# Layer norms and the expert threshold computed on GpSimd instead of ScalarE and VectorE

## The chip, the core and the metric

One NeuronCore of one Trainium2 chip runs the whole program. The metric is the device time of one execution in microseconds; before, the median of three runs is 1113.73 us. TensorE is called PE here, VectorE DVE, ScalarE ACT, GpSimd POOL and SyncE SP, as in the profile.

## The reference

64 sequences of 64 tokens, 128 wide, go through three residual blocks. Each block first takes the layer norm of its input.

```python
def _layernorm(x, axis=-1, eps=1e-05):
    m = jnp.mean(x, axis=axis, keepdims=True)
    v = jnp.var(x, axis=axis, keepdims=True)
    return (x - m) / jnp.sqrt(v + eps)
...
x = x + _L0_xattn_ref(_layernorm(x), ctx_768, Wq, Wk, Wv, Wo, bo)      # cross attention, 16 heads of 64
x = x + _L0_attn_ref(_layernorm(x), Wp, bp, Wv, Wo)                    # causal tree attention, 16 heads
x = x + _L0_ffn_ref(_layernorm(x), Wq, bq, K1, K2, W_up, W_down)       # product-key experts
...
    vals, best = jax.lax.top_k(all_scores, TOPK)       # _L0_ffn_ref: 8 heads, the 10 best of 100 sums
    scores = jax.nn.softmax(vals, axis=-1)
    h = jax.nn.gelu(h, approximate=False) * scores
    out = jnp.einsum('bshk,bshkd->bsd', h, w_up)
```

## The kernel before

The 4096 tokens are worked on as 32 tiles of 128 tokens (two sequences). The work on a tile is cut into about 130 named steps: `x.*` and `y.*` are the cross attention, `t.*` the tree attention, `k.*` the keys of the expert layer and `e.*` its eight heads of 1024 expert sums. Each engine runs its own dictionary of steps, `PE_ORDER`, `ACT_ORDER`, `DVE_ORDER`, `POOL_ORDER`, `SP_ORDER`, written out by hand: the key is the step, the number its lag. Loop `i` of `run` (line 157) goes through the dictionary and does each step for tile `i` minus its lag. So in a full loop every engine works on six or so tiles at once, in a fixed order, and each step waits only for the semaphores of the steps that it needs. There are 32 + 7 loops, of which the first and last ones are thin.

The layer norm, three times a tile (`x`, `t`, `k`):

- DVE takes mean and variance, with the helper `stats` (bn_stats L857, bn_aggr L860, adding eps L862): in `x.stats`, in `y.res` (behind the residual add L906) and in `t.res` (behind L939).
- POOL's `x.root`, `t.root`, `k.root` raise the variance to -0.5 (L1058), wait for that, and multiply it by minus the mean (L1061). Both numbers lie in `rstd`.
- ACT's `x.norm`, `t.norm`, `k.norm` (L686) apply them as scale and bias to the 128x128 tile.
- PE transposes the result (`x.turn` L327, `t.turn` L452, `k.turn` L525).

Behind `k.turn`: ACT's `k.high` (L760) and DVE's `k.low` (L876) split the transposed tile in two fp16 parts, PE's `k.key` makes 512 key scores, DVE's `k.top` takes 16 times the eight largest (L951) and `k.split` (L963, L965) shifts and splits the scores. ACT's `k.shift` (L766) copies them, `e.gelu` (L785 to L787) loads a function table, makes the gelu and loads the first table back, `x.w0`, `x.w1`, `x.w2` (L622) copy queries, `t.sb` (L715) copies the tile that `t.turn` transposed. PE's `x.s0` (L377) needs `x.w0` and `x.w1`; `t.pv` (L462 to L464) comes behind it and feeds ACT's `t.pexp` (L722) and DVE's `t.path` (L919), from which POOL's `t.feat` (L1100, L1104) makes features for PE's `t.fturn`.

The threshold: DVE's `k.cand` finds the 16 best candidates per head with max (L978), match_replace (L983) and max (L988), adds the tenth and the eleventh after the first (L991) and halves the sum (L993) into `cut`. Eight masks `e.w0` to `e.w7` on DVE (L1012) keep the expert weights whose sum is at least `cut`; POOL adds them up in `e.a1` to `e.a7` (L1120). ACT's `k.eb` (L773) takes exponentials of the ten best.

POOL also normalises the attention probabilities, `x.n0` to `x.n3` (L1071), and makes the inner candidates, `k.inner` (L1083, L1089).

Of the kernel before, what the change touches and what calls it, by code (L numbers as in the profile page):

```python
# [29 lines left out]
def build(nc, a):  # L30
# [3 lines left out]
    with ctx:  # L34
# [3 lines left out]
        def sem(name):  # L38
# [36 lines left out]
        rstd = sb("rstd", [128, 3, 2, 2])  # L75
# [53 lines left out]
            dve_path dve_tnorm dve_top dve_split dve_cand dve_zsum pool_inner pool_feat""".split()}  # L129
# [531 lines left out]
        def _(act):  # L661
# [20 lines left out]
            def norm(name, i, src, slots, dst, root, turn):  # L682
                def step(t):
                    act.wait_ge(s[root], t + 1)
                    after(act, turn, t - 2)
                    done(name, act.activation(dst[:, t % 2, :], src[:, t % slots, :], ACT.Identity,  # L686
                                              scale=rstd[:, i, t % 2, 0:1], bias=rstd[:, i, t % 2, 1:2]))
                return step
            steps["x.norm"] = norm("x.norm", 0, x, 2, xn, "x.root", "x.turn")
            steps["t.norm"] = norm("t.norm", 1, x2, 2, xn2, "t.root", "t.turn")  # L690
            steps["k.norm"] = norm("k.norm", 2, x3, 4, xn3, "k.root", "k.turn")

# [107 lines left out]
            steps["x.norm"](0)  # L800
# [4 lines left out]
            run(steps, ACT_ORDER, begun=(("x.norm", 0),), once={ACT_VO: setup_vo, ACT_KEYS: setup_keys})  # L805

        @block.vector
        def _(dve):
# [32 lines left out]
            def setup_down():  # L841
# [9 lines left out]
                                 (("dve_top", 16), ("dve_split", 1), ("dve_cand", 4), ("dve_zsum", 1)))  # L851
# [12 lines left out]
            def x_stats(t):  # L864
                dve.wait_ge(s["ld.x"], 16 * (t + 1))
                after(dve, "x.root", t - 2)
                stat_chain["x.stats"].begin(t)
                stats("x.stats", 0, x[:, t % 2, :], t)
# [30 lines left out]
            def add_cross(t):  # L899
                dve.wait_ge(s["y.out"], t + 1)  # L900
                dve.wait_ge(s["ld.xr"], 16 * (t + 1))
                after(dve, "t.norm", t - 2)
                after(dve, "t.root", t - 2)
# [65 lines left out]
            def candidates(t):  # L969
# [4 lines left out]
                after(dve, "e.w7", t - 4)  # L974
# [14 lines left out]
                lc.link(ins)  # L989
                lc.wait()  # L990
                lc.link(dve.tensor_tensor(cut[:, t % 4, :], best[:, :, TOPK], best[:, :, TOPK + 1], ALU.add))  # L991
                lc.wait()
                done("k.cand", dve.tensor_scalar_mul(cut[:, t % 4, :], cut[:, t % 4, :], 0.5))  # L993
# [49 lines left out]
        def _(pool):  # L1043
# [49 lines left out]
            steps["k.inner"] = inner_sums  # L1093

# [44 lines left out]
    "t.norm": 4, "x.w1": 3, "x.w2": 3, "t.sb": 4, "t.pexp": 4, "t.v": 4, "k.eb": 5, "x.e0": 3, "k.lnz": 5,  # L1139
# [12 lines left out]
    "e.a7": 6, "x.root": 2, "t.feat": 4, "x.n0": 3, "x.n2": 3, "e.a1": 5, "x.n1": 3, "x.n3": 3, "e.a2": 5,  # L1152
    "k.root": 4, "e.a3": 5, "e.a4": 5, "e.a5": 5, "k.inner": 4, "e.a6": 5, "t.root": 3,
# [60 lines left out]
```

## Time and profile before

| | us |
|---|---|
| median of three runs (lowest, highest) | 1113.73 (1105.69, 1114.01) |
| the profiled execution, its own time | 1110.33 |
| its span | 1106.9 |
| busy PE / PE weight loads | 981.0 (89%) / 782.8 (71%) |
| busy ACT | 903.5 (82%) |
| busy DVE | 888.9 (80%) |
| busy POOL | 826.6 (75%) |
| DMA engines, mean | 25 GB/s |

The span is the time from the first to the last instruction of one profiled execution; the execution's own time is 3.4 us more. "Busy" is the time in which an engine had an instruction running, waits left out. The TensorE clock granted is full (tenths 9 or 10) from 100 us to 1020 us.

### The profile page before, as it was taken

The numbers are of one execution on the slowest core, as the hardware profiler recorded it, in microseconds if no ns is written. First come the engines' busy times: TensorE is split into PE (matmuls) and PEld (weight loads), VectorE is DVE, ScalarE is ACT, GpSimd is POOL, SyncE is SP. The second block draws the span as 40 slices with busy tenths as digits, with TensorE's granted clock in tenths as the row PEclk, the third lists the DMA queues.
The fourth block names the chain that finished last, engine by engine and source line by source line (L and its number), as shares of the span: only waits on it lengthen the run. The fifth ranks groups of instructions, "written<-read, shape, count | busy, mean of one in ns | idle before, by whom it ended". The sixth has DMA issues, their size and how long they took to land. (4 is left out here: it accounts for less than half of the span.)

```text
span 1106.9 us, 36026 instructions
## 1 busy us (share of the span) xinstructions
PE 981.0 (89%) x12440; PEld 782.8 (71%) x12440; DVE 888.9 (80%) x2941; ACT 903.5 (82%) x2223; POOL 826.6 (75%) x871
## 2 busy tenths in 40 slices
PE   6869899999999999999999999999999999999865
PEld 5657677777777777777777777777777777777533
DVE  3266898888888888888888888888888888888773
ACT  3557888889898888898988889898888898988752
POOL 0316778788777788877778788777788887777765
PEclk9988999999999999999999999999999999999875
DMA  6000011110001111010011110001111010010000
GB/s 165 13 20 9 20 26 26 26 26 20 15 20 26 25 26 26 20 25 15 19 26 26 25 26 20 17 17 26 26 25 26 21 26 14 20 24 19 13 13 5
DMA packets 70369, 27.27 MB, mean 25 GB/s; under 512 B 47312, under 2 KB 69936, under 8 KB 70192
## 3 DMA queue, kind: packets, MB, share of 16 engines
q1 hardware_dynamic: 69152, 24.58, 9.5%
q8 instruction: 103, 1.69, 0.7%
q14 instruction: 74, 0.61, 0.2%
q10 hardware_dynamic: 1040, 0.39, 0.1%
HBM read 14.47 MB, written 2.10 MB: 15 GB/s over the span
## 5 line engine op out<-in xcount | busy, mean ns | idle before, releaser
L1120 POOL TENSOR_TENSOR wsum<-wsum,mw 128x1024 f32<-128x1024 f32 x192 | 453.1, 2360 | 5.6
L1012 DVE SCALAR_TENSOR_TENSOR mw<-psF,cut,ew 128x1024 f32<-128x1024 f32 x256 | 324.9, 1280 | 38.9 <-ACT ew L795 38.8
L795 ACT ACTIVATE ew<-psF,lnz 128x1024 f32<-128x1024 f32 x256 | 281.5, 1126 | 13.5 <-PE psF L589 10.7
L1071 POOL TENSOR_TENSOR p<-p,rrow 128x512 f32<-128x512 f32 x128 | 131.5, 1038 | 98.4 <-DVE rrow L894 98.4
L705 ACT ACTIVATE p<-psXT,negmax 128x128 f32<-128x128 f32 x512 | 181.8, 383 | 2.2 <-DVE negmax L885 2.1
L589 PE MATMUL psF<-sel,usT 128*128 128x512 f16 x512 | 159.0, 394 | 19.1 <-DVE mw L1012 16.8
L377 PEld LDWEIGHTS psXT<-cT,q 96*128 96x128 f32 x1024 | 131.5, 195 | 60.2 <-DVE q L626 40.1
L377 PE MATMUL psXT<-cT,q 96*128 96x128 f32 x1024 | 142.5, 283 | 31.8 <-DVE q L626 25.9
L705 ACT ACTIVATION_READ_ACCUMULATOR p<-psXT,negmax 128x1 f32 x512 | 115.1, 225 | 0.0
L418 PE MATMUL psXT<-pT,c 128*32 128x384 f32 x768 | 104.7, 501 | 0.6 <-ACT pT L622 0.6
L885 DVE TENSOR_REDUCE negmax<-psXT 128x4 f32<-128x512 f32 x128 | 85.9, 671 | 22.2 <-PE psXT L377 19.4
L420 PE MATMUL psXT<-pT,c 128*32 128x128 f32 x768 | 102.8, 278 | 0.0
L312 PE MATMUL psXT<-xnT,qk 128*96 128x128 f16 x512 | 91.6, 222 | 3.4 <-DVE xnT L876 1.8
L439 PE MATMUL psXT<-vo,uT 128*128 128x128 f32 x768 | 92.6, 277 | 0.0
L314 PE MATMUL psXT<-xnT,qk 128*96 128x128 f16 x512 | 91.4, 222 | 0.0
L313 PE MATMUL psXT<-xnT,qk 128*96 128x128 f16 x512 | 91.4, 222 | 0.0
L439 PEld LDWEIGHTS psXT<-vo,uT 128*128 128x128 f32 x768 | 88.3, 192 | 0.0
L766 ACT ACTIVATE cand<-psXT 128x512 f32<-128x512 f32 x32 | 19.1, 598 | 80.6 <-DVE us L965 80.6
L1058 POOL TENSOR_TENSOR rstd<-mv,halfneg 128x1 f32<-128x1 f32 x96 | 52.8, 550 | 43.0 <-DVE mv L862 42.6
L1120 POOL TENSOR_TENSOR wsum<-mw 128x1024 f32<-128x1024 f32 x32 | 75.5, 2360 | 10.8 <-DVE mw L1012 10.8
L611 PE MATMUL psF<-wup,gT 128*128 128x128 f32 x512 | 70.4, 294 | 11.7 <-DVE mw L1012 10.3
L611 PEld LDWEIGHTS psF<-wup,gT 128*128 128x128 f32 x512 | 64.2, 204 | 18.5 <-DVE mw L1012 16.9
(134 smaller groups left out, 2373.4 us busy)
## 6 DMA issues: line engine op xcount, KB each, us to landing
cT<-cT_dram SPq DMA_DIRECT2D x32, 96.0 KB, 2.0
c<-c_dram SPq DMA_DIRECT2D x32, 96.0 KB, 2.1
x<-x_dram SPq DMA_DIRECT2D x32, 64.0 KB, 2.4
xr<-x_dram SPq DMA_DIRECT2D x32, 64.0 KB, 1.9
y_dram<-y SPq DMA_DIRECT2D x32, 64.0 KB, 1.5
wqT<-wqT_dram SPq DMA_DIRECT2D x1, 512.0 KB, 5.0
wo<-wo_dram SPq DMA_DIRECT2D x1, 512.0 KB, 6.6
wdT<-wdT_dram SPq DMA_DIRECT2D x1, 512.0 KB, 3.5
```

Source lines behind the costliest of these rows:

```text
L312: pe.matmul(out, left[:, 0, :], right[:, 0, :], start=not open_group, stop=False)
L377: mm = pe.matmul(bank[BANK[f"x.s{k}"]][:, i * M:i * M + M], q[:, b, h:h + 2, :].rearrange("c h q -> c (h q)"), cT[:, t % 2, b, :], start=T ...
L418: pe.matmul(to[32 * j:32 * j + 32], cols, probs[:, :, 0:3, :], start=True, stop=True, tile_position=(0, 32 * j))
L420: mm = pe.matmul(to[96:128, :, j, :], cols, probs[:, :, 3, :], start=True, stop=True, tile_position=(0, 96))
L439: mm = pe.matmul(out, uT[:, i, :, :].rearrange("c b q -> c (b q)"), vo[:, i, :], start=False, stop=(i == XH3 - 1))
L589: mm = pe.matmul(bank[BANK[f"e.s{h}"]][:, j * 512:j * 512 + 512], usT[:, t % 4, h, :], sel[:, j * 512:j * 512 + 512], start=True, stop=True)
L611: mm = pe.matmul(bank[BANK["e.out"]][:, 0:D], gT[:, c, :], wup[:, c, :], start=(c == 0), stop=(c == EC - 1))
L705: ins = act.activation(p[:, k, i, :], bank[BANK[f"x.s{k}"]][:, i * M:i * M + M], ACT.Exp, bias=negmax[:, k, i:i + 1], accum_out=rowsum[:, ...
L795: done(f"e.x{h}", act.activation(ew[:, h % NEW, :], bank[BANK[f"e.s{h}"]], ACT.Exp, bias=lnz[:, t % 4, h:h + 1]))
L1012: done(f"e.w{h}", dve.scalar_tensor_tensor(out=mw[:, h % NMW, :], in0=bank[BANK[f"e.s{h}"]], scalar=cut[:, t % 4, h:h + 1], in1=ew[:, h % ...
L1071: done(f"x.n{k}", pool.tensor_tensor(p[:, k, :, :], p[:, k, :, :], rrow[:, k, :].unsqueeze(2).to_broadcast([128, 4, M]), ALU.mult))
L1120: done(f"e.a{h}", pool.tensor_tensor(wsum[:, t % 2, :], mw[:, 0, :] if h == 1 else wsum[:, t % 2, :], mw[:, h % NMW, :], ALU.add))
```

## The change

The three ACT steps `x.norm`, `t.norm`, `k.norm` and the three POOL steps `x.root`, `t.root`, `k.root` become three POOL steps `x.norm`, `t.norm`, `k.norm`: the power as before, a wait for it, and one tensor_scalar that subtracts the mean from the 128x128 tile and multiplies by the root. They stand where the roots stood. The add and the halving of the threshold leave DVE's `k.cand` and become a POOL step `k.cut`, between `e.a7` and `x.norm`, one loop behind `k.cand`. The masks wait for `k.cut` besides. The first `x.norm` is no longer issued ahead of the setup on ACT.

```diff
         @block.scalar
-            def norm(name, i, src, slots, dst, root, turn):
-                def step(t):
-                    act.wait_ge(s[root], t + 1)
-                    after(act, turn, t - 2)
-                    done(name, act.activation(dst[:, t % 2, :], src[:, t % slots, :], ACT.Identity,
-                                              scale=rstd[:, i, t % 2, 0:1], bias=rstd[:, i, t % 2, 1:2]))
-                return step
...
         @block.vector
             def candidates(t):
...
-                after(dve, "e.w7", t - 4)
+                after(dve, "k.cut", t - 1)
...
                 for h in range(FH):
                     ins = dve.max(best[:, h, 8:16], cand2[:, h, :])
-                lc.link(ins)
-                lc.wait()
-                lc.link(dve.tensor_tensor(cut[:, t % 4, :], best[:, :, TOPK], best[:, :, TOPK + 1], ALU.add))
-                lc.wait()
-                done("k.cand", dve.tensor_scalar_mul(cut[:, t % 4, :], cut[:, t % 4, :], 0.5))
+                done("k.cand", ins)
...
             def mask(h):
                 def step(t):
                     dve.wait_ge(s[f"e.x{h}"], t + 1)
+                    dve.wait_ge(s["k.cut"], t + 1)
...
         @block.gpsimd
-            def root(name, i, stats, norm):
+            def layer_norm(name, i, src, slots, dst, stats, turn):
+
                 def step(t):
                     pool.wait_ge(s[stats], t + 1)
-                    after(pool, norm, t - 2)
-                    l = root_chain[name]
+                    after(pool, turn, t - 2)
+                    l = norm_chain[name]
                     l.begin(t)
                     l.link(pool.tensor_tensor(rstd[:, i, t % 2, 0:1], mv[:, i, t % 2, 1:2], halfneg[:], ALU.pow))
                     l.wait()
                     pool.nop(nofuse=True)
-                    done(name, pool.tensor_scalar(rstd[:, i, t % 2, 1:2], mv[:, i, t % 2, 0:1],
-                                                  rstd[:, i, t % 2, 0:1], -1.0, ALU.mult, ALU.mult))
+                    done(name, pool.tensor_scalar(dst[:, t % 2, :], src[:, t % slots, :], mv[:, i, t % 2, 0:1],
+                                                  rstd[:, i, t % 2, 0:1], ALU.subtract, ALU.mult))
...
+            def middle(t):
+
+                pool.wait_ge(s["k.cand"], t + 1)
+                after(pool, "e.w7", t - 4)
+                lcut.begin(t)
+                pool.nop(nofuse=True)
+                lcut.link(pool.tensor_tensor(cut[:, t % 4, :], best[:, :, TOPK], best[:, :, TOPK + 1], ALU.add))
+                lcut.wait()
+                done("k.cut", pool.tensor_scalar_mul(cut[:, t % 4, :], cut[:, t % 4, :], 0.5))
+            steps["k.cut"] = middle
...
 POOL_ORDER = {
-    "e.a7": 6, "x.root": 2, "t.feat": 4, "x.n0": 3, "x.n2": 3, "e.a1": 5, "x.n1": 3, "x.n3": 3, "e.a2": 5,
-    "k.root": 4, "e.a3": 5, "e.a4": 5, "e.a5": 5, "k.inner": 4, "e.a6": 5, "t.root": 3,
+    "e.a7": 6, "k.cut": 5, "x.norm": 2, "t.feat": 4, "x.n0": 3, "x.n2": 3, "e.a1": 5, "x.n1": 3, "x.n3": 3,
+    "e.a2": 5, "k.norm": 4, "e.a3": 5, "e.a4": 5, "e.a5": 5, "k.inner": 4, "e.a6": 5, "t.norm": 3,
 }
```

The order of the instructions on each engine, in a full loop. ACT before, around `k.norm`: two exponentials of expert sums (`ew`), the norm of the third block (`xn`, L686), a copy of the mix (`uT`) and `k.high` (`xn3T`).

```order
L795 ACTIVATE ew<-psF,lnz 128x1024 [waits e_w1,k_lnz,e_s5]
L795 ACTIVATE ew<-psF,lnz 128x1024 [waits e_w2,k_lnz,e_s6]
L686 ACTIVATE xn<-x,rstd 128x128 [waits k_turn,k_root]
L622 ACTIVATE uT<-psXT 128x6x64 [waits y_out,y_m1]
L760 ACTIVATE xn3T<-psXT 128x128 [waits e_hid,k_key,k_turn]
L622 ACTIVATE uT<-psXT 128x6x64 [waits y_out,y_m3]
```

ACT now, at the same place:

```order
L784 ACTIVATE ew<-psF,lnz 128x1024 [waits e_w1,k_lnz,e_s5]
L784 ACTIVATE ew<-psF,lnz 128x1024 [waits e_w2,k_lnz,e_s6]
L622 ACTIVATE uT<-psXT 128x6x64 [waits y_out,y_m1]
L749 ACTIVATE xn3T<-psXT 128x128 [waits e_hid,k_key,k_turn]
L622 ACTIVATE uT<-psXT 128x6x64 [waits y_out,y_m3]
```

Only the norm has gone; the rest follows in the same order. ACT before, around `t.norm`: the table load behind the gelu, the query copies `x.w0`, `x.w1`, `x.w2` (`q`), the norm between the first two, and `t.sb` (`xn2T`).

```order
L787 ACT_TABLE_LOAD
L622 ACTIVATE q<-psXT 96x4x2x64 [waits x_s2,x_s0,x_q0]
L686 ACTIVATE xn<-x,rstd 128x128 [waits t_turn,t_root]
L622 ACTIVATE q<-psXT 96x4x2x64 [waits x_s2,x_s0,x_q1]
L622 ACTIVATE q<-psXT 96x4x2x64 [waits x_s3,x_s1,x_q2]
L715 ACTIVATE xn2T<-psXT 128x128 [waits t_pv,t_turn]
```

ACT now, at the same place:

```order
L776 ACT_TABLE_LOAD
L622 ACTIVATE q<-psXT 96x4x2x64 [waits x_s2,x_s0,x_q0]
L622 ACTIVATE q<-psXT 96x4x2x64 [waits x_s2,x_s0,x_q1]
L622 ACTIVATE q<-psXT 96x4x2x64 [waits x_s3,x_s1,x_q2]
L704 ACTIVATE xn2T<-psXT 128x128 [waits t_pv,t_turn]
```

`x.w1` now stands directly behind `x.w0`. POOL before, from `e.a6` to `t.feat`: sums of masked weights (`wsum`), the roots of the second and the first block (`rstd`), and the first instruction of the features (`path`).

```order
L1120 TENSOR_TENSOR wsum<-wsum,mw 128x1024 [waits e_w6,e_a5]
L1058 TENSOR_TENSOR rstd<-mv,halfneg 128x1 [waits t_norm,y_res]
L1061 TENSOR_SCALAR rstd<-mv,rstd 128x1 [waits pool_t_root]
L1120 TENSOR_TENSOR wsum<-wsum,mw 128x1024 [waits e_w7,e_a6]
L1058 TENSOR_TENSOR rstd<-mv,halfneg 128x1 [waits x_norm,x_stats]
L1061 TENSOR_SCALAR rstd<-mv,rstd 128x1 [waits pool_x_root]
L1100 TENSOR_SCALAR path<-path 128x80 [waits t_path,t_fturn]
```

POOL now, at the same place:

```order
L1117 TENSOR_TENSOR wsum<-wsum,mw 128x1024 [waits e_w6,e_a5]
L1044 TENSOR_TENSOR rstd<-mv,halfneg 128x1 [waits t_turn,y_res]
L1047 TENSOR_SCALAR xn<-x,mv,rstd 128x128 [waits pool_t_norm]
L1117 TENSOR_TENSOR wsum<-wsum,mw 128x1024 [waits e_w7,e_a6]
L1087 TENSOR_TENSOR cut<-best 128x8 [waits k_cand,e_w7]
L1089 TENSOR_SCALAR cut<-cut 128x8 [waits pool_cut]
L1044 TENSOR_TENSOR rstd<-mv,halfneg 128x1 [waits x_turn,x_stats]
L1047 TENSOR_SCALAR xn<-x,mv,rstd 128x128 [waits pool_x_norm]
L1097 TENSOR_SCALAR path<-path 128x80 [waits t_path,t_fturn]
```

The second instruction of each root has become one over the 128x128 tile, and the two of `k.cut` stand between `e.a7` and `x.norm`. On PE the order is the same; on DVE only the two threshold instructions are gone.

## Rows read from the trace of the kernel before

**Rows 1.** Busy us (instructions) in one loop: PE, PEld, DVE, ACT, POOL; clock, DMA.

```profile
502.53:534.41 31.88, 29.43 (x388) 23.69 (x387) 27.37 (x91) 27.90 (x71) 25.79 (x27) 1.00 0.10 23
```

**Rows 2.** Timeline of ACT, first and last full loops: start, us, instruction, [idle before <-releaser].

```profile
119.70 0.22 ACT L722 ACTIVATE psXT<-psXT 128x80 f32<-128x80 f32 x1 [1.22 <-PE psXT L464]
...
1012.24 0.22 ACT L722 ACTIVATE psXT<-psXT 128x80 f32<-128x80 f32 x1 [1.22 <-PE psXT L464]
```

**Rows 3.** Timeline of ACT, one full loop, 502.5 to 536 us.

```profile
519.60 0.51 ACT L686 ACTIVATE xn<-x,rstd 128x128 f32<-128x128 f32 x1
...
520.59 0.28 ACT L760 ACTIVATE xn3T<-psXT 128x128 f16<-128x128 f32 x1
...
526.51 0.60 ACT L766 ACTIVATE cand<-psXT 128x512 f32<-128x512 f32 x1 [2.43 <-DVE us L965]
...
531.25 0.48 ACT L686 ACTIVATE xn<-x,rstd 128x128 f32<-128x128 f32 x1
531.64 1.06 ACT L622 ACTIVATE q<-psXT 96x512 f32<-96x512 f32 x2
...
534.09 0.22 ACT L722 ACTIVATE psXT<-psXT 128x80 f32<-128x80 f32 x1 [1.22 <-PE psXT L464]
```

**Rows 4.** Timeline of DVE, the same loop.

```profile
518.75 1.28 DVE L1012 SCALAR_TENSOR_TENSOR mw<-psF,cut,ew 128x1024 f32<-128x1024 f32 x1 [0.42 <-ACT ew L795]
...
522.57 1.66 DVE L951 MAX8 top<-psXT 128x8 f32<-128x32 f32 x16
...
525.79 0.69 DVE L965 SCALAR_TENSOR_TENSOR us<-psXT,us 128x512 f16<-128x512 f32 x1
...
533.05 0.17 DVE L991 TENSOR_TENSOR cut<-best 128x8 f32<-128x8 f32 x1
```

**Rows 5.** Timeline of PE, the same loop.

```profile
515.71 0.30 PE L513 MATMUL psXT<-ident,actx 128*128 128x128 f32 x1 [0.29 <-DVE actx L929]
...
520.25 0.30 PE L525 MATMUL psXT<-ident,xn 128*128 128x128 f32 x1 [0.26 <-ACT xn L686]
520.39 0.59 PE L589 MATMUL psF<-sel,usT 128*128 128x512 f16 x2
...
531.57 0.22 PE L314 MATMUL psXT<-xnT,qk 128*96 128x128 f16 x1
...
532.36 1.13 PE L377 MATMUL psXT<-cT,q 96*128 96x128 f32 x8 [0.18 <-ACT q L622]
```

**Rows 6.** Timeline of POOL, the same loop.

```profile
518.42 0.55 POOL L1058 TENSOR_TENSOR rstd<-mv,halfneg 128x1 f32<-128x1 f32 x1 [0.25 <-DVE mv L862]
...
529.83 0.55 POOL L1058 TENSOR_TENSOR rstd<-mv,halfneg 128x1 f32<-128x1 f32 x1
...
533.82 0.27 POOL L1061 TENSOR_SCALAR rstd<-mv,rstd 128x1 f32<-128x1 f32 x1 [0.17 <-POOL rstd L1058]
536.19 0.26 POOL L1100 TENSOR_SCALAR path<-path 128x80 f32<-128x80 f32 x1 [2.11 <-DVE path L919]
```

**Rows 7.** Groups by form, POOL: busy us, mean ns of one, idle before and releaser.

```profile
L1071 POOL TENSOR_TENSOR p<-p,rrow 128x512 f32<-128x512 f32 x128 | 131.5, 1038 | 98.4 <-DVE rrow L894 98.4
...
L1100 POOL TENSOR_SCALAR path<-path 128x80 f32<-128x80 f32 x32 | 8.3, 258 | 75.3 <-DVE path L919 75.3
L1104 POOL TENSOR_TENSOR feat<-feat,path 128x16 f32<-128x16 f32 x32 | 7.9, 248 | 2.7
```

**Rows 8.** The chain that ended last, in order of time, thin loops: start, us, what.

```profile
1058.24 0.02 issue
1058.26 0.30 DVE x L939
...
1060.45 0.50 ACT xn L686
...
1073.64 0.18 DVE cut L991
```

**Rows 9.** All masks of the run: ns min/median/max, first and last start.

```profile
L1012 DVE SCALAR_TENSOR_TENSOR mw<-psF,cut,ew x256: 1271/1283/1286, 90.2 to 1091.5; 128x1024 f32<-128x1024 f32 x128
```

More of the change, by code:

```diff
@@ L74, in build @@
         mv = sb("mv", [128, 3, 2, 2])
-        rstd = sb("rstd", [128, 3, 2, 2])
+        rstd = sb("rstd", [128, 3, 2, 1])
         xn = sb("xn", [128, 2, D])
@@ L128, in build @@
             setup_ps setup_sb key_sb parts_done split_done
-            dve_path dve_tnorm dve_top dve_split dve_cand dve_zsum pool_inner pool_feat""".split()}
+            dve_path dve_tnorm dve_top dve_split dve_cand dve_zsum pool_inner pool_cut pool_feat""".split()}
         block = ctx.enter_context(nc.Block())
@@ L680, in _ @@
             copies(act, steps, ACT_ORDER)
-            def norm(name, i, src, slots, dst, root, turn):
-                def step(t):
-                    act.wait_ge(s[root], t + 1)
-                    after(act, turn, t - 2)
-                    done(name, act.activation(dst[:, t % 2, :], src[:, t % slots, :], ACT.Identity,
-                                              scale=rstd[:, i, t % 2, 0:1], bias=rstd[:, i, t % 2, 1:2]))
-                return step
-            steps["x.norm"] = norm("x.norm", 0, x, 2, xn, "x.root", "x.turn")
-            steps["t.norm"] = norm("t.norm", 1, x2, 2, xn2, "t.root", "t.turn")
-            steps["k.norm"] = norm("k.norm", 2, x3, 4, xn3, "k.root", "k.turn")
             def x_high(t):
@@ L799, in _ @@
                 steps[f"e.x{h}"] = exp_sums(h)
-            steps["x.norm"](0)
             for j in range(4):
@@ L804, in _ @@
                                ACT.Copy, scale=QKSCALE).then_inc(own["setup_sb"], 1)
-            run(steps, ACT_ORDER, begun=(("x.norm", 0),), once={ACT_VO: setup_vo, ACT_KEYS: setup_keys})
+            run(steps, ACT_ORDER, once={ACT_VO: setup_vo, ACT_KEYS: setup_keys})
         @block.vector
@@ L850, in _ @@
             ltop, lsp, lc, lz = (Chain(dve, own[n], k) for n, k in
-                                 (("dve_top", 16), ("dve_split", 1), ("dve_cand", 4), ("dve_zsum", 1)))
+                                 (("dve_top", 16), ("dve_split", 1), ("dve_cand", 2), ("dve_zsum", 1)))
             stat_chain = {n: Chain(dve, sem("dve_" + n.replace(".", "_")), k)
@@ L865, in x_stats @@
                 dve.wait_ge(s["ld.x"], 16 * (t + 1))
-                after(dve, "x.root", t - 2)
+                after(dve, "x.norm", t - 2)
                 stat_chain["x.stats"].begin(t)
@@ L902, in add_cross @@
                 after(dve, "t.norm", t - 2)
-                after(dve, "t.root", t - 2)
                 l = stat_chain["y.res"]
@@ L1048, in _ @@
             steps = {}
-            root_chain = {n: Chain(pool, sem("pool_" + n.replace(".", "_")), 1) for n in ("x.root", "t.root", "k.root")}
+            lcut = Chain(pool, own["pool_cut"], 1)
+            norm_chain = {n: Chain(pool, sem("pool_" + n.replace(".", "_")), 1) for n in ("x.norm", "t.norm", "k.norm")}
             li, lf = (Chain(pool, own[n], k) for n, k in (("pool_inner", 1), ("pool_feat", DEPTH)))
-            def root(name, i, stats, norm):
+            def layer_norm(name, i, src, slots, dst, stats, turn):
                 def step(t):
                     pool.wait_ge(s[stats], t + 1)
-                    after(pool, norm, t - 2)
-                    l = root_chain[name]
+                    after(pool, turn, t - 2)
+                    l = norm_chain[name]
                     l.begin(t)
@@ L1060, in step @@
                     pool.nop(nofuse=True)
-                    done(name, pool.tensor_scalar(rstd[:, i, t % 2, 1:2], mv[:, i, t % 2, 0:1],
-                                                  rstd[:, i, t % 2, 0:1], -1.0, ALU.mult, ALU.mult))
-                return step
-            steps["x.root"] = root("x.root", 0, "x.stats", "x.norm")
-            steps["t.root"] = root("t.root", 1, "y.res", "t.norm")
-            steps["k.root"] = root("k.root", 2, "t.res", "k.norm")
+                    done(name, pool.tensor_scalar(dst[:, t % 2, :], src[:, t % slots, :], mv[:, i, t % 2, 0:1],
+                                                  rstd[:, i, t % 2, 0:1], ALU.subtract, ALU.mult))
+                return step
+            steps["x.norm"] = layer_norm("x.norm", 0, x, 2, xn, "x.stats", "x.turn")
+            steps["t.norm"] = layer_norm("t.norm", 1, x2, 2, xn2, "y.res", "t.turn")
+            steps["k.norm"] = layer_norm("k.norm", 2, x3, 4, xn3, "t.res", "k.turn")
             def norm(k):
@@ L1138 @@
 ACT_ORDER = {
-    "t.norm": 4, "x.w1": 3, "x.w2": 3, "t.sb": 4, "t.pexp": 4, "t.v": 4, "k.eb": 5, "x.e0": 3, "k.lnz": 5,
[4 rows of a table removed]
[4 rows of a table added]
 }
```

8 rows, old and new, of the table ACT_ORDER are left out of this document.

## The prediction

> **What bounds the kernel now.** I read the busy shares first. In a full loop of 31.88 us PE works 29.43, DVE 27.37, ACT 27.90 and POOL 25.79 [rows 1]: no engine is full, so the period is set by a ring of waits, and the question is which ring and what the change takes from it. The activation `t.pexp` starts at 119.70 and again at 1012.24 [rows 2]; 892.54 us at 31.88 are 28 full loops, which carry nearly the whole effect.
>
> Next I read the four compute engines over one loop, 502.5 to 534.4, and asked at each idle gap what ended it. The ring:
> - ACT has no gap from `t.pexp` (at 502.2, and 534.09 a loop later) to `k.high` at 520.59 [rows 3]. On the way stands `k.norm` at 519.60.
> - `k.high` frees DVE's `k.low` and PE's `k.key`; DVE goes on with `e.w6`, the 16 maxima of `k.top` at 522.57, and ends `k.split` at 525.79 + 0.69 = 526.48 [rows 4].
> - ACT has waited 2.43 us for just that, and starts `k.shift` at 526.51 [rows 3]. Two table loads, the gelu, `x.w0`, `t.norm` at 531.25 and `x.w1` at 531.64 follow without a gap.
> - PE's `x.s0` waits 0.18 us for `x.w1` and starts at 532.36 [rows 5]; `t.pv` follows, ACT waits 1.22 us for it and starts `t.pexp` at 534.09 [rows 3]. The ring closes after 31.88 us.
>
> POOL is not in the ring: it stands idle for 2.11 us before `t.feat` [rows 6]. The third norm, `x.norm`, stands behind `k.high` and before the 2.43 us gap, so it costs nothing today.
>
> **The change part by part.**
>
> *ACT loses three activations a loop.* In a busy queue one takes the distance between neighbours: 531.64 - 531.25 = 0.39 us, though each is listed with about 0.5 [rows 3]. `x.norm` gives nothing (the 2.43 us gap becomes longer). The other two lie on the ring.
>
> *At `k.norm`* the activation frees 0.39 us, but `k.high` also needs PE's transpose `k.turn`. That waited 0.26 us for the normalised tile and ran at 520.25 [rows 5]; before it PE's work has followed on since `t.cturn` at 515.71 (behind a 0.29 us wait for DVE), and nothing of that moves. So `k.turn` can come at 519.99, 0.26 earlier. Behind it `e.s7`, now at 520.39, waits for the mask `e.w5`, which ends at 518.75 + 1.28 = 520.03 [rows 4]; with the 0.14 us that PE shows between a releaser's end and its matmul, `e.s7` starts at 520.17, 0.22 earlier. `x.p0`, `k.key` and so `k.top` follow. I take 0.22 us here, not 0.39. Is the tile there in time? POOL starts the root at 518.42 [rows 6]; 0.55 for the power, 0.17 wait and 0.35 for the new instruction (below) end at 519.49, and PE could start at 519.63. It is, with 0.36 to spare.
>
> *At `t.norm`* the full 0.39 us goes: `x.w1` starts 0.22 + 0.39 = 0.61 earlier, and `x.s0` could start at 531.75. The others it needs: PE's queries end at 531.57 + 0.22 = 531.79 [rows 5], shifted to 531.57; the transpose `t.turn` starts then, and a matmul behind a transpose starts 0.14 later (520.25 to 520.39), so 531.71. That is just not the bound. `t.turn` needs POOL's `t.norm`: 529.83, plus 0.08 from `k.norm`, plus 0.55 + 0.17 + 0.35 = 530.98 [rows 6], 531.12 on PE. It holds with 0.4 us to spare. So `t.pexp` comes 0.61 us earlier each loop.
>
> *The new POOL instruction* (128x128, one tensor input, two scalars in memory) is not in the trace. The nearest row is the 128x80 scalar form, 258 ns; with both inputs tensors, 128x16 costs 248 and 128x512 costs 1038, that is 1.6 ns an element, so 48 elements more than 80 make at most 0.33 [rows 7]. Bounds: 0.26 below, 0.43 above (248 and 112 elements more of the two-tensor kind), and 1.04, far away, the 128x512 row itself. I take 0.35, nearest the first row; against the 128x1 form at 533.82 that it replaces (0.27 [rows 6]) this is 0.08 more, three times a loop.
>
> That a norm on POOL costs no more than a small instruction speaks against a general warning. The Trainium skill, "GPSIMD Engine Reference", section "Engine selection", sends elementwise work to VectorE, GpSimd being about half as fast with two inputs, but calls one-input work roughly line-rate. At that page's 1.2 GHz the 128 elements are 0.11 us beyond the fixed cost, an estimate; no run so far shows the instruction. By it the sum above stays.
>
> *The threshold on POOL:* an 8-element add (at most 0.25, the 128x16 row), a 0.17 wait and a scalar form (0.26): 0.68 us [rows 6, 7]. It stands after `e.a7`, ending about 533.2, where the maxima of `k.cand`, ending at 533.0, are just done; shifted by 0.22 they are earlier still. The next reader, mask `e.w2`, stands eight DVE instructions further on, so this wait costs nothing. Behind it on POOL are `x.norm` (used a loop later) and `t.feat`. POOL's last small instruction ended at 533.82 + 0.27 = 534.09; now 0.24 + 0.68 later, 535.01. `t.feat`, at 536.19 because DVE's path comes then, will want to start at 535.58. So 0.57 us remain. That is the cover of all the POOL work; what is added beyond it makes `t.feat` late and then `t.fturn` on PE.
>
> *DVE loses* the add and the multiplication of the threshold, two of 0.17 from 533.05, with their waits some 0.4 us [rows 4]. The next, the maxima `x.x0`, needs `x.s0`, whose 1.13 us end at 533.49 [rows 5], so they hid nothing but 0.06 us of waiting. In the loop they are worth 0. The eight masks get a third wait (`k.cut`); where DVE already stands with three waits, at the residual add behind `t.out`, it starts 0.02 us after its releaser all the same [rows 8]. I take 0, at worst 0.05 at two or three masks beside the ring.
>
> The shared memory interface is the other worry. Masks that read one tile in SBUF and one in PSUM take 1271 to 1286 ns over all 256, beside a POOL that works 25.79 of 31.88 us [rows 1, 9]: no contention shows. The Trainium skill, "GPSIMD Engine Reference", section "Key points", expects it only with two SBUF inputs or a 2-port mode of VectorE; by that rule the new POOL reads could stretch VectorE's small SBUF operations, which are some 0.3 us each and few. That would change the sum by less than 0.1 us a loop.
>
> *Outside the full loops.* At the end, `k.norm` is in the chain (0.50 at 1060.45) and so are the two threshold instructions (from 1073.64 on, 0.39 with the gaps) [rows 8]. The first saves 0.50 + 0.02 - 0.08 = 0.4, the second 0.4. At the start some three thin loops hold one or both norms: 1.1 us by estimate.
>
> **Sum:** 28 x 0.61 = 17.1, plus 0.8 and 1.1: 19.0 us. The profiled execution took 1110.33 us, 3.4 outside its span and all; less 19.0 that is 1091.3. The median of the three runs is 1113.73, 3.4 above the profiled run, so in its terms 1094.7. I predict 1095. The three runs reach from 1105.69 to 1114.01; about 1%, 11 us, is what a measurement can tell from no change.
>
> **The rivals.**
> 1. *Only one of the two savings arrives.* For it: within 0.3 us of the ring run PE's route (0.26 idle before `k.turn`, 0.18 before `x.s0`) and the start of `x.s0` is only 0.04 clear of PE's. Against: I followed these and found them in step. If `k.norm` gives nothing, 28 x 0.39 + 1.9 = 12.8 us, 1101; if `t.norm` gives nothing, 28 x 0.22 + 1.9 = 8.1 us, 1106. Chance 0.22, about half of it under 1%.
> 2. *Slower: POOL becomes the bound.* One mechanism: the new instruction is much dearer, because of its two scalars in memory. The extra d counts twice up to `t.norm`: POOL's tile came at 530.82 against ACT's at 531.74, so from d = 0.46 (an instruction of 0.73 us) `t.turn` is no earlier than now. It counts three times up to `t.feat`, where 2.11 - 0.68 = 1.43 us were free, to be passed at d = 0.48. At 1.04 us (d = 0.77) `t.feat` is 3 x 0.77 - 1.43 = 0.9 late, less some 0.3 of room before `t.fturn`: 0.6 x 28 = 17 us slower, 1130. Against: the 128x80 form at 258 ns. The Trainium skill, "GPSIMD Engine Reference", section "Engine selection", with its preference for VectorE speaks the same way as this rival. Chance 0.08.
> 3. *No effect:* some chain that I missed holds the period at 31.88, for instance masks handed over later by the third wait, which runs beside the ring through `x.r0` and POOL's `x.n1` to PE's `x.p1`. Only the ends gain: 1112. Chance 0.10.
>
> **How the numbers follow.** The forecast has 0.60 and is faster by 1.7%. With half of rival 1 (0.11) faster has 0.70; same is the other half and most of rival 3, 0.20; slower is rival 2 and a rest of 0.02, 0.10. The range: the forecast's own is 1088 to 1100 (0.45 to 0.8 us a loop, the latter if PE overlaps more than I allow). It is widened to 1084 because one run of before was 8 us under the median, and to 1111 for rival 1 and a part of rival 3.
>
> **What would show it.** Right: loops of 31.27 us between two `t.pexp`; `k.turn` at 0.26 less distance from `t.cturn`; POOL's norm instruction near 0.35 us; ACT down by 3 x 0.49 busy a loop, with its wait before `k.shift` grown by 0.4 to 0.6; POOL's gap before `t.feat` down from 2.11 to about 0.6. Wrong: a gap on PE before `t.turn` or `t.fturn` that POOL ends, a POOL norm above 0.7 us, or DVE masks starting more than 0.05 us behind ACT.

## The result, and the profile after

The changed kernel takes 1102.05 us (median of 20 runs), the kernel before 1109.43 (20 runs): a ratio of 0.9942, 95% interval 0.9927 to 0.9958. It is faster by 0.6%, where I had forecast 1.7% (1095 us), and by less than the 1% that I had called the limit of "no change". The three runs that I had to predict from had a median 4 us above that of the twenty.

The first row to read is the one I had to estimate: the new instruction, all 96 of them.

```profile
L1047 POOL TENSOR_SCALAR xn<-x,mv,rstd x96: 797/797/1027, 4.7 to 1052.3; 128x128 f32<-128x128 f32 x96
```

Its columns are ns min/median/max, first and last start. I had taken 350 ns, with 0.26 to 0.43 as near bounds. The timeline of ACT has `t.pexp` twice in a typical full loop; [rows 3] is its counterpart.

```profile
211.42 0.22 ACT L711 ACTIVATE psXT<-psXT 128x80 f32<-128x80 f32 x1 [1.34 <-PE psXT L464]
...
243.07 0.22 ACT L711 ACTIVATE psXT<-psXT 128x80 f32<-128x80 f32 x1 [1.34 <-PE psXT L464]
```

The loop is 31.65 us, not 31.27. Busy time in that loop (columns as in [rows 1]):

```profile
211.42:243.07 31.65, 29.48 (x387) 23.57 (x386) 26.96 (x90) 26.98 (x66) 27.85 (x30) 1.00 0.10 23
```

ACT lost 0.92 us and POOL gained 2.06 against [rows 1]. I had forecast 1.47 for ACT, three times the listed 0.49; neighbouring activations overlap, so each takes away less busy time than its own length. Who is late is on the timeline of PE at `k.turn`, `t.turn` and `x.s0`:

```profile
229.13 0.30 PE L525 MATMUL psXT<-ident,xn 128*128 128x128 f32 x1
...
241.12 0.30 PE L452 MATMUL psXT<-ident,xn 128*128 128x128 f32 x1 [0.45 <-POOL xn L1047]
241.35 1.13 PE L377 MATMUL psXT<-cT,q 96*128 96x128 f32 x8
```

`t.turn` waits 0.45 us for POOL, one of the rows that I had named as the sign of failure. (`x.s0`, which waited 0.18 us for ACT in [rows 5], has no wait here.) The timeline of POOL, the counterpart of [rows 6], says why.

```profile
213.63 0.26 POOL L1097 TENSOR_SCALAR path<-path 128x80 f32<-128x80 f32 x1
...
227.46 0.56 POOL L1044 TENSOR_TENSOR rstd<-mv,halfneg 128x1 f32<-128x1 f32 x1
228.19 0.80 POOL L1047 TENSOR_SCALAR xn<-x,mv,rstd 128x128 f32<-128x128 f32 x1 [0.18 <-POOL rstd L1044]
228.96 7.25 POOL L1117 TENSOR_TENSOR wsum<-wsum,mw 128x1024 f32<-128x1024 f32 x3
236.16 0.32 POOL L1069 TENSOR_TENSOR tops<-top 128x80 f32<-128x80 f32 x1
236.56 0.61 POOL L1075 TENSOR_TENSOR cand<-tops 128x32 f32<-128x32 f32 x3
237.13 2.35 POOL L1117 TENSOR_TENSOR wsum<-wsum,mw 128x1024 f32<-128x1024 f32 x1
239.44 0.56 POOL L1044 TENSOR_TENSOR rstd<-mv,halfneg 128x1 f32<-128x1 f32 x1
240.18 0.80 POOL L1047 TENSOR_SCALAR xn<-x,mv,rstd 128x128 f32<-128x128 f32 x1 [0.18 <-POOL rstd L1044]
```

From `k.norm` to the end of `t.norm` POOL has no gap but the 0.18 us between a norm's two instructions. Its last longer gap lies before `x.n3`, which waits 0.65 us for DVE's reciprocal L882 and starts 12.6 us after `t.pexp`. So POOL is now part of the ring: `x.n3`, `e.a2`, `k.norm`, three sums, `k.inner`, `e.a6`, `t.norm`, then PE's `t.turn`, `x.s0`, `t.pv` and ACT's `t.pexp`. The 2.11 us that POOL idled before `t.feat` are gone (no bracket at 213.63).

**Where the time went, by the profiled executions.** I split each span at the third `t.pexp` and at the one 28 loops later. Before: 119.70, 892.54, 94.66 us. After: 115.65, 887.98, 94.17. So of 9.1 us, 4.6 came from the 28 loops (0.16 each on average, since a few of them are longer than 31.65), 4.05 from the thin loops at the start and 0.5 from the end. The start is not to be put down to the norms. In its last thin loop PE ran at a mean granted clock of 0.90 before and 0.98 after:

```profile
85.73:119.70 33.97, 29.65 (x363) 23.66 (x362) 25.91 (x89) 28.19 (x70) 25.76 (x27) 0.90 0.09 20
```

```profile
83.91:115.65 31.74, 26.98 (x363) 21.25 (x362) 25.57 (x87) 26.82 (x67) 25.98 (x25) 0.98 0.09 21
```

The first is before, the second after. This stretch differs by some us between executions of the same instructions: the kernel before, run again, reached its third `t.pexp` at 118.46 us, where it had been 119.70, and the kernel of the probe below, which is the changed one up to its end, at 117.55, where that had been 115.65. So I compare the kernels by their full loops.

### The profile page after: what moved, and what is told of

Read it like the earlier page. It is cut to its first block and busy times, and to the rows that moved or that the text cites. A ratio compares the mean times of both kernels' runs of the same rounds, so it can differ in the third digit from the quotient of the medians.

```text
span 1097.8 us, 35846 instructions
## 1 busy us (share of the span) xinstructions
PE 980.3 (89%) x12440; PEld 778.7 (71%) x12440; DVE 876.6 (80%) x2877; ACT 873.4 (80%) x2127; POOL 892.2 (81%) x935
## 5 line engine op out<-in xcount | busy, mean ns | idle before, releaser
L1047 POOL TENSOR_SCALAR xn<-x,mv,rstd 128x128 f32<-128x128 f32 x96 | 76.9, 801 | 17.3 <-POOL rstd L1044 17.3
L622 ACT ACTIVATE pT<-psXT 128x512 f32<-128x512 f32 x128 | 74.1, 605 | 9.6 <-PE psXT L396 8.8
```

## The experiments

Loop is the distance of two `t.pexp` in the commonest full loop, mean the average over the same 28. Both are read from one profiled execution of each kernel. The expectations below speak of `arz`: in the kernel before, DVE stood idle for 0.25 us ahead of this reciprocal (L927) in 25 of its 32 loops, and the profile names nobody that it waited for. The last two runs are about this stall.

| kernel | loop, us | mean, us | ratio to before, 95% interval |
|---|---|---|---|
| before | 31.88 | 31.88 | |
| changed | 31.65 | 31.71 | 0.9942 (0.9927 to 0.9958) |
| threshold alone on POOL | 31.69 | 31.72 | 0.9972 (0.9947 to 0.9998) |
| norms alone on POOL | 32.33 | 32.42 | 1.0164 (1.0107 to 1.0221) |
| changed, POOL reordered | 31.20 | 31.26 | 0.9816 (0.9767 to 0.9865) |
| changed, cheaper norm instruction | 31.01 | 31.05 | 0.9753 (0.9707 to 0.9800) |
| norms alone, threshold sum a reduction | 32.07 and 32.85 | 32.42 | 1.0159 (1.0110 to 1.0208) |
| norms alone, threshold one reduction | 31.70 | 31.76 | 0.9963 (0.9952 to 0.9975) |
| reordered, `t.norm` back on ACT | 31.58 | 31.62 | one run, 1103.00 us |
| reordered, norm by an addition | 31.04 | 31.05 | 0.9775 (0.9755 to 0.9795) |
| before again | 31.85 | 31.86 | one run, 1106.45 us |
| before, one empty DVE instruction a loop | 31.72 | 31.75 | one run, 1105.93 us |

**The threshold alone.** The kernel before, with `k.cut` of the change and its waits in the masks.

```diff
-    "e.a7": 6, "x.root": 2, "t.feat": 4, ...
+    "e.a7": 6, "k.cut": 5, "x.root": 2, "t.feat": 4, ...
```

> The kernel before with the threshold alone moved to POOL; the norms stay on ACT. Theory A (the changed kernel's gain comes from the two norm activations that left ACT, and was capped by POOL's 0.80 us norms): the ring still runs through ACT's k.norm and t.norm, so a full loop stays at 31.88 us, or 31.72 if the 0.25 us stall of DVE before arz, which is in most loops of the kernel before and in none of the changed one, depends on DVE's instruction stream; the time is the same within 0.5%. Theory B (it is the shorter DVE that gave the gain, the norms gave nothing): the loop is 31.65 us as in the changed kernel, and the ratio to before is 0.994.

Measured: a loop of 31.69 us, ratio 0.9972, and the 25 stalls before `arz` are gone. The loop fits A with the stall gone (31.72); its distance from B's 31.65 is too small to decide. The last run, which takes only the stall out of the kernel before, has 31.72 as well: the threshold by itself, the third wait of the masks included, neither gives nor costs anything that these loops show. The averages, 31.72 here and 31.71 in the changed kernel, say more: the norms on POOL, as the change writes them, added next to nothing to this kernel's loops.

**The norms alone.** The changed kernel with the two threshold instructions back on DVE.

```diff
-                done("k.cand", ins)
+                lc.link(ins)
+                lc.wait()
+                lc.link(dve.tensor_tensor(cut[:, t % 4, :], best[:, :, TOPK], best[:, :, TOPK + 1], ALU.add))
+                lc.wait()
+                done("k.cand", dve.tensor_scalar_mul(cut[:, t % 4, :], cut[:, t % 4, :], 0.5))
```

> The changed kernel with the threshold back on DVE. Theory A: POOL's ring, from e.a2 over k.norm, three sums, k.inner, e.a6 and t.norm to PE's t.turn, sets the loop with or without k.cut, because k.cut stands outside it: 31.65 us without the stall before arz, 31.82 with it, PE idle 0.4 us before t.turn on POOL's account; ratio to before 0.994 to 0.998. Theory B: without the shorter DVE the loop is back at 31.88.

Both missed: 32.33 us, slower than before by 1.6%. The cause is one instruction that neither theory had looked at, DVE's add L978 (all 32; columns as above). The second row is the same add in the kernel before.

```profile
L978 DVE TENSOR_TENSOR cut<-best x32: 171/1395/1478, 82.4 to 1087.5; 128x8 f32<-128x8 f32 x32
```

```profile
L991 DVE TENSOR_TENSOR cut<-best x32: 170/171/275, 82.7 to 1073.6; 128x8 f32<-128x8 f32 x32
```

An add of 8 elements in each partition takes 1.4 us; before it took 0.17 [rows 4]. The timelines of DVE and of POOL at that place:

```profile
699.50 1.13 DVE L978 TENSOR_TENSOR cut<-best 128x8 f32<-128x8 f32 x1
700.67 0.17 DVE L980 TENSOR_SCALAR cut<-cut 128x8 f32<-128x8 f32 x1
```

```profile
698.25 2.36 POOL L1108 TENSOR_TENSOR wsum<-wsum,mw 128x1024 f32<-128x1024 f32 x1
```

POOL's sum `e.a7` ends at 700.61, the add at 700.63. So it is in the other loops: in 30 of the 32 the add starts 0.98 to 1.45 us before the end of `e.a7` and ends 0.02 to 0.04 us after it. Before, `e.a7` ran from 28.57 to 30.92 us after `t.pexp` and the add began at 30.85: it came just as the sum ended. Three of its 32 adds began 0.18 to 0.25 us before the end of the sum and took 0.20, 0.26 and 0.28 us, ending with it, so the first sign of this stood in the trace that I predicted from. The norms move `e.a7` to 30.18 and its end to 32.5, on top of the add. The maxima behind the add are then late, ACT waits for them (0.33 us at `x.e0`), and the ring grows.

**POOL reordered.** Two steps of the changed kernel stand elsewhere.

```diff
-    "e.a7": 6, "k.cut": 5, "x.norm": 2, "t.feat": 4, "x.n0": 3, "x.n2": 3, "e.a1": 5, "x.n1": 3, "x.n3": 3,
-    "e.a2": 5, "k.norm": 4, "e.a3": 5, "e.a4": 5, "e.a5": 5, "k.inner": 4, "e.a6": 5, "t.norm": 3,
+    "e.a7": 6, "k.cut": 5, "t.feat": 4, "x.norm": 2, "x.n0": 3, "x.n2": 3, "e.a1": 5, "x.n1": 3, "x.n3": 3,
+    "e.a2": 5, "k.norm": 4, "e.a3": 5, "e.a4": 5, "e.a5": 5, "k.inner": 4, "t.norm": 3, "e.a6": 5,
```

> The changed kernel with two POOL steps in other places: t.norm before e.a6 in place of behind it, x.norm behind t.feat in place of before it. Nothing is computed otherwise. Theory A: t.norm's tile is ready some 2 us earlier, so PE no longer waits for POOL before t.turn, and the ring is the one that I forecast for the change: 0.56 to 0.61 us less than 31.72, a loop of 31.1 to 31.2 us; 28 loops by 0.5 us from 31.65 are 14 us, so about 0.982 of before. Theory C (PE's own queue or a DVE handoff is what holds 31.65, POOL only looks late): the loop stays at 31.5 to 31.7 and the ratio at 0.994.

Measured: 31.20 us and 0.9816, as theory A had it. Theory C is out. POOL at `t.norm`:

```profile
675.48 0.56 POOL L1044 TENSOR_TENSOR rstd<-mv,halfneg 128x1 f32<-128x1 f32 x1 [0.48 <-DVE mv L850]
676.22 0.80 POOL L1047 TENSOR_SCALAR xn<-x,mv,rstd 128x128 f32<-128x128 f32 x1 [0.18 <-POOL rstd L1044]
```

The tile is ready at 27.8 us after `t.pexp` (649.21), where it was 29.6; `t.turn` follows PE's queries at 29.12 without a wait. The two exchanges were made together; what `x.norm` behind `t.feat` gives by itself no run shows.

**The price of the instruction.** Eight forms on scratch tiles at the end of the program, where nothing else runs on POOL.

```diff
...
+            form(lambda: pool.tensor_scalar(pb[:, 0:128], pa[:, 0:128], m, r, ALU.subtract, ALU.mult))
+            form(lambda: pool.tensor_scalar(pb[:, 0:128], pa[:, 0:128], m, r, ALU.mult, ALU.add))
+            form(lambda: pool.tensor_scalar(pb[:, 0:128], pa[:, 0:128], r, -1.0, ALU.mult, ALU.mult))
+            form(lambda: pool.tensor_scalar(pb[:, 0:128], pa[:, 0:128], 2.0, -1.0, ALU.mult, ALU.add))
...
```

> The changed kernel, and when POOL has nothing more to do it runs eight forms of instruction three times each on scratch tiles, with a wait between them; they compute nothing that is used. It measures what the forecast took at 0.35 us. Theory P (two scalars in memory cost by the element, some 5 to 6 ns): two memory scalars take 0.80 us over 128 elements, 0.5 over 64, 1.4 over 256, and immediates 0.3. Theory S (it is the subtraction): multiply-and-add with two memory scalars takes 0.35 and only subtract-and-multiply 0.80. Theory F (a fixed cost of two scalars in memory): 0.8 at every width from 1 to 256.

The rows of the tile that they write, in that order, then the first form at 64, 1 and 256 columns, and a two-tensor multiplication:

```profile
L1138 POOL TENSOR_SCALAR pb<-pa,mv,rstd x3: 792/793/802, 1092.0 to 1093.8; 128x128 f32<-128x128 f32 x3
L1139 POOL TENSOR_SCALAR pb<-pa,mv,rstd x3: 447/447/448, 1094.7 to 1095.8; 128x128 f32<-128x128 f32 x3
L1140 POOL TENSOR_SCALAR pb<-pa,rstd x3: 366/371/373, 1096.4 to 1097.3; 128x128 f32<-128x128 f32 x3
L1141 POOL TENSOR_SCALAR pb<-pa x3: 297/298/298, 1097.8 to 1098.5; 128x128 f32<-128x128 f32 x3
L1142 POOL TENSOR_SCALAR pb<-pa,mv,rstd x3: 572/574/580, 1098.9 to 1100.3; 128x64 f32<-128x64 f32 x3
L1143 POOL TENSOR_SCALAR pb<-pa,mv,rstd x3: 364/370/399, 1101.0 to 1101.9; 128x1 f32<-128x1 f32 x3
L1144 POOL TENSOR_SCALAR pb<-pa,mv,rstd x3: 1220/1246/1246, 1102.4 to 1105.1; 128x256 f32<-128x256 f32 x3
L1145 POOL TENSOR_TENSOR pb<-pa,rstd x3: 398/399/399, 1106.4 to 1107.3; 128x128 f32<-128x128 f32 x3
```

Theory S, in kind: at 128 columns and with the same two memory scalars, subtract-and-multiply takes 793 ns and multiply-and-add 447, though S had 350 for the latter. The memory scalars cost about 75 ns each at this width (298, 371, 447); the form with the subtraction costs 3.4 ns an element ((1246 - 370) / 255). F is out by the 370 ns at one column, P by the 447: it had the dear price for any form with two memory scalars. What this probe leaves open is whether the subtraction is dear or any form that adds before it multiplies; a run below settles it.

**The cheaper form in the kernel.** The norms compute x * root + mean, not the layer norm; it is a measure of time.

```diff
-                    ... src[:, t % slots, :], mv[:, i, t % 2, 0:1], rstd[:, i, t % 2, 0:1], ALU.subtract, ALU.mult)
+                    ... src[:, t % slots, :], rstd[:, i, t % 2, 0:1], mv[:, i, t % 2, 0:1], ALU.mult, ALU.add)
```

> The changed kernel in which the three POOL norms multiply by the root and add the mean (447 ns in the probe) where they subtract the mean and multiply by the root (796 ns). This is another value than the layer norm, and so a measure of time alone: the instruction costs about what I had forecast. Theory A (the forecast failed by this one price): k.norm and t.norm are 0.35 us each shorter, t.norm's tile comes 0.70 us earlier at PE where the changed kernel waits 0.45 for it, so POOL leaves the ring and the loop falls from 31.65 to 31.2 us, the ratio to before to 0.983. Theory C (something else also caps the changed kernel at this order of POOL): the loop stays above 31.45.

31.01 us and 0.9753: A, and more than its 31.2. With this one price changed, POOL's place in the order is as in the changed kernel and the loop is 0.64 us shorter. The reordered kernel had stopped at 31.20 because its `k.norm` still held `k.turn`, which came 17.75 us after `t.pexp`; here it comes at 17.54.

**One input in place of two.** To see what holds DVE in the norms-alone kernel, the sum became a reduction.

```diff
-                lc.link(dve.tensor_tensor(cut[:, t % 4, :], best[:, :, TOPK], best[:, :, TOPK + 1], ALU.add))
+                lc.link(dve.reduce_sum(cut[:, t % 4, :], best[:, :, TOPK:TOPK + 2], AX.X))
```

> The kernel with only the norms on POOL, where DVE's threshold add took 1.28 us in place of 0.18 and the loop 32.33 us. Here DVE makes the same sum as a reduction over the two neighbouring values, one input where the add has two. Theory K (a DVE instruction with two inputs in SBUF waits until POOL's running two-input instruction is over): the reduction takes about 0.2 us beside the same POOL work, and the loop falls to what POOL's ring gives, 31.65 to 31.8 us, ratio 0.994 to 0.999. Theory L (DVE there waits for something else, or any DVE instruction on these addresses is held): the reduction too takes over 1 us and the loop stays at 32.3.

The loop is as slow on average (32.42 us), but another instruction is held. The reduction and the halving behind it on DVE's timeline, and POOL's sum:

```profile
667.97 0.17 DVE L978 TENSOR_REDUCE cut<-best 128x8 f32<-128x16 f32 x1
668.17 0.85 DVE L980 TENSOR_SCALAR cut<-cut 128x8 f32<-128x8 f32 x1
```

```profile
666.64 2.35 POOL L1108 TENSOR_TENSOR wsum<-wsum,mw 128x1024 f32<-128x1024 f32 x1
```

Beside the same sum the reduction takes its usual 0.17 us. The halving, which has one input, starts after it and ends at 669.02, when the sum ends (668.99). K was right on the reduction, but it had only instructions with two inputs held, and so its 31.65 to 31.8 us for the loop missed.

Nor is every scalar form from SBUF to SBUF held. In the norms-alone kernel the addition of eps to the variance, L850 over one column, kept its time in all 96, this one inside the POOL sum under it:

```profile
L850 DVE TENSOR_SCALAR mv<-mv x96: 153/154/156, 3.5 to 1073.0; 128x1 f32<-128x1 f32 x96
...
694.99 0.15 DVE L850 TENSOR_SCALAR mv<-mv 128x1 f32<-128x1 f32 x1
```

```profile
694.43 2.36 POOL L1108 TENSOR_TENSOR wsum<-wsum,mw 128x1024 f32<-128x1024 f32 x1
```

The multiplication by -1 over one column, in a kernel below, takes 142 to 146 ns in all 96 as well. What sets the halving over 8 columns apart, other than its width, no run here asks.

**Reduction only.** The threshold is the tenth best itself, by one reduction; the middle between two values is left out.

```diff
-                lc.link(dve.tensor_tensor(cut[:, t % 4, :], best[:, :, TOPK], best[:, :, TOPK + 1], ALU.add))
-                lc.wait()
-                done("k.cand", dve.tensor_scalar_mul(cut[:, t % 4, :], cut[:, t % 4, :], 0.5))
+                done("k.cand", dve.tensor_reduce(cut[:, t % 4, :], best[:, :, TOPK:TOPK + 1], AX.X, ALU.max))
```

> The kernel with only the norms on POOL, its threshold made by one DVE reduction alone (the tenth best itself, in place of the middle between the tenth and the eleventh, so the masks at the edge can differ; taken for time). With the sum as a reduction, that took 0.17 us, but the halving behind it, 0.17 us in the kernel before, took 1.08 us and ended with POOL's sum e.a7. Theory K (while POOL runs a long two-input instruction DVE's additions of two SBUF tensors and its SBUF-to-SBUF scalar forms are held until it is over, reductions and maxima aren't): no DVE instruction is held, and the loop is set by POOL's ring, 31.65 to 31.8 us; ratio 0.993 to 0.998. Theory L (DVE is held there whatever it runs): the reduction takes over 1 us and the loop stays at 32.1 to 32.3.

31.70 us, 0.9963, the threshold instruction not held (165 to 168 ns in all 32), and `t.turn` waiting 0.46 us for POOL as in the changed kernel: as K has it for this kernel, and POOL's ring again. So with the norms on POOL, the threshold in DVE's old form costs 0.63 us a loop (32.33 less 31.70); the plain 0.17 us of the second instruction is in that.

**One ACT norm put back.** In the reordered kernel `t.norm` is an activation again.

```diff
-    "x.w1": 3, "x.w2": 3, "t.sb": 4, ...
+    "t.norm": 4, "x.w1": 3, "x.w2": 3, "t.sb": 4, ...
```

> The reordered kernel with one step put back: t.norm again on ACT between x.w0 and x.w1, its root on POOL with the small second instruction. Theory A (each ACT activation on the ring is worth its distance of 0.39 us): the loop is 31.20 + 0.39 = 31.59 us. Theory C (the ring does not run through these ACT steps): it stays at 31.2.

31.58 us, 0.38 more than the reordered kernel. The 0.39 us of the forecast for `t.norm` stand. (The second instruction of the norm on POOL is the small one again, as in the kernel before.)

**A correct cheap norm.** The reordered kernel, with the mean negated on DVE.

```diff
                 done(name, dve.tensor_scalar_add(mv[:, i, t % 2, 1:2], mv[:, i, t % 2, 1:2], 1e-5))
+                dve.tensor_scalar_mul(nm[:, i, t % 2, :], mv[:, i, t % 2, 0:1], -1.0).then_inc(negated[i], 1)
...
-                    ... mv[:, i, t % 2, 0:1], rstd[:, i, t % 2, 0:1], ALU.subtract, ALU.mult)
+                    ... nm[:, i, t % 2, :], rstd[:, i, t % 2, 0:1], ALU.add, ALU.mult)
```

> The reordered kernel, with the norm made of cheaper operations and the same value: DVE takes the mean times -1 behind its eps addition (one more 128x1 instruction, about 0.15 us, three times a loop), and POOL adds that and multiplies by the root where it subtracted the mean. Theory S (on POOL it is the subtraction that is dear): the norm takes 0.45 us in place of 0.80, k.norm no longer holds PE's k.turn by 0.2 us, and the loop goes from 31.20 to 31.0 us as with the multiply-and-add form; ratio to before about 0.976. Theory T (any form in which the addend comes first is dear, or DVE's three instructions cost more than they give): the loop stays at 31.2 or rises to 31.4.

```profile
L1051 POOL TENSOR_SCALAR xn<-x,nm,rstd x96: 451/452/640, 4.6 to 1032.7; 128x128 f32<-128x128 f32 x96
```

The norm takes 452 ns, the loop 31.04 us, and the median is 1081.96 us against 1107.86 for before beside it: 0.9775, the fastest kernel here that computes the layer norms. Theory S holds and T is out: negation and addition are cheap where the subtraction is not.

**The stall before `arz`.** In the kernel before, DVE idled 0.25 us ahead of the reciprocal L927 in 25 loops, with no releaser (the profile writes "issue").

```profile
514.55 0.18 DVE L894 RECIPROCAL rrow<-rowsum 128x4 f32<-128x4 f32 x1
514.98 0.26 DVE L927 RECIPROCAL arz<-psXT 128x16 f32<-128x16 f32 x1 [0.25 <-issue]
```

Two runs asked about it; the second adds one empty instruction.

```diff
                 ltn.begin(t)
+                dve.nop(nofuse=True)
```

> The kernel before once more, for the stall of 0.25 us before DVE's arz that stood in 25 of its 32 loops and made them 31.88 us in place of 31.72. Theory M (it belongs to this program): again 25 stalls at arz. Theory N (it belongs to that one execution): none or few, and full loops of 31.7 us. The changed kernel's gain per loop would then be 0.05 to 0.1 us against such an execution, not 0.23.

> The kernel before with one empty instruction on DVE in each loop ahead of arz, where two executions of it had the same 25 stalls of 0.25 us. Theory O (the stall comes from how the waits or the stream of instructions fall at this place): it goes or moves, and a full loop is 31.7 us. Theory Q (the data that arz reads are not there earlier): arz starts as late as before, the loop stays at 31.85.

Run again, the kernel before has the same 25 stalls and loops of 31.85: it belongs to the program. With the empty instruction they are gone and the loop is 31.72, which is theory O:

```profile
639.65 0.18 DVE L894 RECIPROCAL rrow<-rowsum 128x4 f32<-128x4 f32 x1
639.75 0.26 DVE L928 RECIPROCAL arz<-psXT 128x16 f32<-128x16 f32 x1
```

The stall sits on the ring through `t.cturn` and ACT's `t.csb`. None of the other kernels here has it, the norms-alone kernel included, in which DVE computes the same as before. What makes it is not known.

## Why the prediction was wrong, point by point

**The ring and its two exits: right.** `t.norm` on ACT is worth 0.39 us (measured 0.38, 31.58 less 31.20), and the ring runs where I drew it. When POOL was in time, the loop fell to 31.04 and 31.01, even below my 31.27. Of that, 0.16 us is the stall, which I had not seen; against the 31.72 without it the fall is 0.68 and 0.71, where I had 0.61. What `k.norm` and `x.norm` are worth one by one no run shows. One step was off without harm: I had `x.s0` 0.14 us behind the start of `t.turn`, and it comes 0.23 behind it in the changed kernel.

**The failed step** is the one headed "The new POOL instruction": I took 0.35 us, and it measured 0.80. I took the price of a 128x80 multiply-and-add with immediate scalars for a subtract-and-multiply with scalars in memory. Two memory scalars more add 0.15 us, the subtraction 0.35. The 0.11 us that I had estimated beside the sum for 128 elements beyond the fixed cost is not borne out either: 793 less 370 ns is 0.42. The outer bound, 1.04, held the value; I had set it aside for its distance and gave it a chance of 0.08. With 0.80, `k.norm` and `t.norm` together bring POOL's tile 0.9 us later than I had it, against a cover of 0.45. By my own sum that makes a loop of 31.27 + 0.9 - 0.45 = 31.72 us, near the 31.65 measured. With the instruction at 0.45 us and nothing else changed the loop was 31.01: in this order of POOL's steps it was the price that put POOL in the ring.

**Rival 2 had the right mechanism and the wrong sign.** It said that at 0.73 us for the instruction `t.turn` would be no earlier than now. It is so: 29.70 us after `t.pexp`, before 29.68 (the row below, `t.pexp` at 502.2).

```profile
531.88 0.30 PE L452 MATMUL psXT<-ident,xn 128*128 128x128 f32 x1
```

But `x.s0` had stood 0.48 us behind the start of `t.turn`, waiting for `x.w1`; with `x.w1` early it follows after 0.23. These 0.25 us, less the 0.02 by which `t.turn` is later, are the 0.23 of the typical loop. Against the kernel before without the stall, where `t.turn` starts at 29.52, it is 0.18 later, and only 0.07 is left. `t.feat` comes 0.1 us later than before, and no wait of `t.fturn` for it is in the trace, so the third term of the rival stayed off.

**Rival 1 gave nearly the right number by accident.** Its 1101 us, or its 0.22 us a loop with only `k.norm` saved, look like the 1102.05 and the 0.23 measured. But its reason, PE's own route, did not act: it is POOL that PE waits for, and reordered the loop fell to 31.20. It is luck as well that the result lies within my 1084 to 1111, whose upper part stands there for rivals 1 and 3.

**The threshold: wrong, and by luck harmless.** I priced its move at nothing, which is what it gives without the norms apart from the stall (31.69 against 31.72). With the norms it is what keeps the change from being 1.6% slower. I had read 256 masks for signs of contention, found none, and put the rest below 0.1 us; the three slower threshold adds in the same trace I did not look at. The masks have one input in PSUM; the threshold add has both in SBUF, which is just the case that the Trainium skill names ("GPSIMD Engine Reference", section "Key points", with the 2-port mode). The trace agrees, and shows how much: the 0.17 us instruction lasts until POOL's sum ends, up to 1.48 us. I cited the rule and did not go through DVE's instructions with it.

**Most of the gain in the loops was not forecast at all.** 0.16 us of a typical loop is the stall, which one empty instruction removes as well. Against the kernel before without it (31.72), the changed kernel gains 0.07 us a typical loop (0.04 by the averages, 31.75 and 31.71), and the reordered one 0.52. I had read that row as an ordinary wait for DVE (the 0.29 us at [rows 5]).

**The ends.** I gave 1.9 us; the two profiled spans show 4.5, of which 2.2 lie in the one thin loop where PE's clock differs. As executions of the same instructions differ by 1.2 and 1.9 us at this place, these runs neither confirm nor refute my figure.

## What to carry to other kernels

An operation moved to another engine is priced by its exact form: the operations it applies and where its scalars lie, not its shape. Where no row has that form, the distant bound belongs in the range, and a probe of a few instructions settles it. Before work is added to GpSimd, list the VectorE instructions that will now run beside its long ones, and look first at small ones with two SBUF inputs and at scalar forms from SBUF to SBUF over more than one column: here they were held, where reductions, maxima and one-column forms were not. Before a gain is put down to a change, look in the trace of before for idle time with no releaser; here such a stall was 0.16 of the 0.23 us that a typical loop gained. In a ring, a step that others wait for goes ahead of the long ones that nobody waits for: two pairs of names exchanged in an order gave 1.3%, twice what moving the work had given.

## What the runs showed of the hardware that I had not expected

- GpSimd, 128x128 fp32 with two memory scalars: subtract-and-multiply 793 ns, multiply-and-add 447, add-and-multiply 452.
- A VectorE instruction over 128x8 elements that takes 171 ns alone took up to 1478 ns beside a 2.36 us GpSimd sum of two tensors and ended with it, as an add of two SBUF inputs and as a scalar multiplication from SBUF to SBUF (up to 1262); reductions and maxima beside the same sum kept their time, and so did scalar additions over 128x1 beside other POOL sums (153 to 156 ns in all 96).
- One empty instruction ahead of a VectorE reciprocal removed a 0.25 us stall that had no releaser, in all 25 loops that had it.
